# Row fetches by byte offsets, a tile in 12 and 14 sets, and a read-back with sets between its segments

## The chip, the core and the metric

One core of a Trainium2 chip runs the whole program. Its engines work side by side and meet only at semaphores: TensorE (PE in the profile), VectorE (DVE), ScalarE (ACT), GpSimd (POOL) and SyncE (SP). SyncE and ScalarE also issue direct DMA transfers, GpSimd issues indirect ones (a row of HBM for each of 128 partitions). The metric is device time in microseconds (us) of one execution; lower is better.

## What is computed

A layer of a graph network over 12,500 nodes of 256 features and 200,000 edges: a normalised row of each node goes through a weight matrix, is gathered along the edges, scaled and summed by destination; a linear attention over all nodes is added; then a mixture of 8 experts (the best 2 per node) is added.

```
xn = _layernorm(x, axis=-1)
HW = xn @ gnn_W
msgs = edge_vals[:, None] * HW[col]                       # row, col = src, dst
AHW = jax.ops.segment_sum(msgs, row, num_segments=12500)
x = x + (AHW + gnn_b) + linear_attention(xn)              # 8 heads of 32, elu(.)+1, bias mix_bproj
x = x + experts(_layernorm(x))                            # top 2 of 8, relu, 256 -> 512 -> 256
```

## The kernel before

**Sorting** (to about 677 us). The edges are sorted by destination block. A table of `xn @ gnn_W` is written to HBM (`h_table`, 12,544 rows of 1 KB), and the sorted edges are scattered to HBM as lists.

**Read-back** (about 680 to 776 us). The lists come back in 13 segments of 128 tiles (a tile is 128 edges of one destination block of 128 nodes). For each segment SyncE loads a list (L544), TensorE joins it (L1238), ScalarE copies it (`joined`, L965), TensorE turns it (L1280), ScalarE copies it again (`found`, L982). VectorE unpacks the segments in four parts, of 1, 4, 4 and 4 segments, into `records` (L1860 to L1877): the row to gather, the destination in the block, the weight. In this time ScalarE also fills the accumulator `acc` with the summed biases, in 14 pieces (L975), and TensorE turns the four weight matrices of the attention (L1267), which ScalarE copies (L972).

**Sets** (about 700 to 2770 us). 1,660 tiles are worked in 415 sets of four. For a tile, GpSimd gathers 128 rows of `h_table` into `message` (L757, one indirect DMA per tile, a ring of four sets); VectorE makes a selection matrix (`select`, L1815); TensorE multiplies the two (`aggregate`, L1258); VectorE adds the product to `acc` (L1823). GpSimd may be four sets ahead of TensorE: before set k it waits until set k - 4 is multiplied.

**Direct fetches.** In some sets the fourth tile is not gathered by GpSimd. SyncE or ScalarE fetches its 128 rows one by one, each by a direct DMA of 1 KB whose address comes from a register (L452), into `fetched`, two buffers for each queue. SyncE fetches one tile while 16 sets pass (25 tiles in all), ScalarE one while 20 pass (19 tiles). The row numbers stand in `fetch_row`, which is ready after the last segment; a queue loads eight of them into registers at a time (`TENSOR_LOAD`, L47), bounds them (L48) and issues eight transfers. `fetch_span` deals the rows out evenly: of span sets, the rows from 128·s/span to 128·(s + count)/span, rounded down, are fetched beside sets s to s + count.

**Attention beside the sets.** Sets 8 to 154 go with 49 context units, three sets each; sets 155 to 158 with the step between; sets 159 to 403 with 49 mix units, five sets each; 11 sets follow. In a context unit ScalarE takes `exp` and `relu` of the keys (L997, L998), copies the values (L1007), and then issues the unit's share of row transfers; in a mix unit `exp` and `relu` of the queries (L1026, L1027), then the rows. SyncE loads a unit's inputs (L563, in the mix also L575) once TensorE is through with the buffer, then issues its rows. Both queues work in order: what comes behind the rows of a unit waits until they are issued. VectorE needs ScalarE's `relu` within each unit (L1950), TensorE needs `v_sb` and SyncE's inputs.

**Experts** (about 2770 us to the end). Not touched by the change.

Of the kernel before, what the change touches and what calls it, by code (L numbers as in the profile page):

```python
# [50 lines left out]
def gps_layer(nc, x, src, dst, edge_weight, gnn_W, gnn_b, mix_Wq, mix_Wkv, mix_Wproj, mix_bproj,  # L51
# [4 lines left out]
    F32, BF16, I32 = mybir.dt.float32, mybir.dt.bfloat16, mybir.dt.int32  # L56
# [48 lines left out]
    AHEAD_SETS = 5  # L105
# [4 lines left out]
    SP_SPAN, SP_SET = 16, 27  # L110
    ACT_SPAN, ACT_SET = 20, 37
# [35 lines left out]
    with ExitStack() as whole:  # L147
# [16 lines left out]
        tiles_f = sb("tiles_f", [P, 4], F32)  # L164

# [34 lines left out]
        gnn_w = sb("gnn_w", [P, KC, C], F32, sorting)  # L200
        x_buf = sb("x_buf", [P, 14, 2 * C], F32, sorting)
# [30 lines left out]
        w_nat = lent[:, 0:8 * C].rearrange("p (a c) -> p a c", c=C)  # L232
        bias_in = lent[:, 8 * C:10 * C].rearrange("p (a c) -> p a c", c=C)
# [12 lines left out]
        bias_row = sb("bias_row", [P, C], F32, early)  # L246
# [71 lines left out]
        s_first_w = sem("s_first_w")  # L318
        s_x_group = [sem(f"s_x_group{i}") for i in range(3)]
# [170 lines left out]
        def _(sp):  # L490
# [23 lines left out]
            sp.wait_ge(s_block_dram, 16)  # L514
            for j in range(3, XGROUPS):
                sp.wait_ge(s_x_read, j - 2)
                load_group(j)
# [32 lines left out]
            sp.dma_start(bias_in[:, 0, :], gnn_b.partition_broadcast(P)).then_inc(s_first_w, 16)  # L550
            sp.dma_start(bias_in[:, 1, :], mix_bproj.partition_broadcast(P)).then_inc(s_first_w, 16)
# [25 lines left out]
            row_registers = [sp.alloc_register(f"row_{i}") for i in range(8)]  # L577
# [88 lines left out]
        def _(pool):  # L666
# [42 lines left out]
            def pass_gate():  # L709

                pool.sem_inc(s_passed, 1)
            pool.wait_ge(s_zeroed, 16 * G8)
# [12 lines left out]
            for slot in range(4):  # L725
                pool.wait_ge(s_xt_out[slot], STORED[slot])
                pool.wait_ge(s_h_out[slot], STORED[slot])
            pool.iota(iota_tile[:, :], [[1, TC]], base=0, channel_multiplier=0, allow_small_or_imprecise_dtypes=True)
# [19 lines left out]

            pool.wait_ge(s_first_w, 48)
            steps.done(pool.tensor_tensor(bias_row[:, :], bias_in[:, 0, :], bias_in[:, 1, :], ALU.add))  # L750
            steps.settle()
            pool.engine_nop().then_inc(s_late, 1)
# [82 lines left out]
        def _(act):  # L835
# [122 lines left out]


# [7 lines left out]
            def copy_weights():  # L967
                for i in range(4):
                    act.wait_ge(s_wt_psum, i + 1)
                    ps = bank[i][:, :].rearrange("p (k a n) -> p k a n", k=KC, a=2)  # L970
# [3 lines left out]
            def fill_acc(piece):  # L974
                act.activation(acc[:, 7 * piece:7 * piece + 7, 0:C], bias_row[:, :].unsqueeze(1).to_broadcast([P, 7, C]),  # L975
                               ACT.Copy).then_inc(s_acc_made, 1)
            join(0)
            for seg in range(RSEG):
                if seg + 1 < RSEG:
                    join(seg + 1)  # L980
                act.wait_ge(s_back_psum, seg + 1)
                act.activation(found_bf[:, seg * P:(seg + 1) * P, :],  # L982
                               bank[4 + seg % 2][:, :].rearrange("p (c t) -> p t c", c=PIECES), ACT.Copy).then_inc(s_back_out, 1)
                if seg == 1:
                    act.wait_ge(s_late, 3)
                if seg == 6:
                    copy_weights()
                for piece in range(2 * seg - 2, 2 * seg):
                    if 0 <= piece < NB // 7:
                        fill_acc(piece)  # L990


            def split_k(unit, first=False):
# [4 lines left out]
                act.activation(relu_kq[:, :], bank[4][:, :], ACT.Relu).then_inc(s_k_split, 1)  # L998
                act.wait_ge(s_v_psum, unit + 1)
# [9 lines left out]
            row_registers = [act.alloc_register(f"row_{i}") for i in range(8)]  # L1009
# [94 lines left out]
        def _(pe):  # L1104
# [156 lines left out]
            def turn_weights():  # L1261
                pe.wait_ge(s_tile_row, -(-TC // 512))
                pe.wait_ge(s_wload, 16 * 3)
                for i in range(4):
                    for k in range(KC):
                        for a in range(2):
                            last = nc.tensor.transpose(bank[i][:, (k * 2 + a) * P:(k * 2 + a + 1) * P],  # L1267
# [3 lines left out]
            for seg in range(RSEG):  # L1271
                if seg + 1 < RSEG:
                    join(seg + 1)
                if seg == 5:
                    turn_weights()
# [261 lines left out]
        def _(dve):  # L1537
# [274 lines left out]
            dve.wait_ge(s_late, 2)  # L1812
# [40 lines left out]

            for nth, (a, b) in enumerate(PARTS):
# [33 lines left out]
                elif nth == 1:  # L1888
# [10 lines left out]
            for k in range(AHEAD_SETS, RING):  # L1899
                set_turn(k)  # L1900
            dve.wait_ge(s_fetch_psum, 1)
            V.tensor_copy(fetch_row[:, :], bank[6][0:FETCHED, 0:P]).then_inc(s_fetch_row, 1)
# [33 lines left out]
            dve.wait_ge(s_late, 3)  # L1936
            dve.wait_ge(s_acc_made, NB // 7)
# [352 lines left out]
```

## Time and profile before

| | |
|---|---|
| median of three runs | 3810.78 us (3808.42 to 3811.88) |
| the profiled execution | 3811.51 us, of it 3809.8 us from the first to the last instruction |
| PE busy | 2769.5 us (73%) |
| DVE busy | 2526.5 us (66%) |
| POOL busy | 2461.2 us (65%) |
| ACT busy | 635.4 us (17%) |
| row transfers issued by SyncE and by ScalarE | 3200 and 2432, 1 KB each |

The shares are averages over stages with different limits. Issuing a DMA, loading a register and waiting for a semaphore are not counted as busy: a queue may be full although its engine reads as idle. In lists of groups the columns are line, engine, operation, output and input, count, then busy us and mean ns, then idle us just before them and what ended most of it; names that end in q (SPq, ACTq) are an engine's sequencer.

### The profile page before, as it was taken

Reading aid. Unit: us, or ns where it says so; the run is one execution under the profiler, and the core shown is the slowest. Engines: PE = TensorE matmul, PEld = TensorE weight load, DVE = VectorE, ACT = ScalarE, POOL = GpSimd, SP = SyncE. Lnnn points to the kernel's source line nnn. Section 1 sums busy time; section 2 is a strip of 40 time slices with the busy share of each in tenths; the row PEclk is TensorE's granted clock in tenths of the full one; section 3 lists DMA queues with packets and bytes.
Section 4 is the critical chain, followed back from the end, with each engine's and each line's share of the span. In section 5 each row is a group of like instructions: output and inputs, shape, how many; then the busy total and the mean of one; then the engine's idle time right before and its main releaser. Section 6 shows DMA issues by size and latency. Waiting matters only on the chain. (4 is left out here: it accounts for less than half of the span.)

```text
span 3809.8 us, 70900 instructions
## 1 busy us (share of the span) xinstructions
PE 2769.5 (73%) x16407; PEld 2275.1 (60%) x16408; DVE 2526.5 (66%) x6338; ACT 635.4 (17%) x1335; POOL 2461.2 (65%) x2387
## 2 busy tenths in 40 slices
PE   1457676577777776667666777666654999999998
PEld 1346666366556565555555555555432888888887
DVE  8999998355555555777777777777683544454444
ACT  8212222311111110000000000000032221122221
POOL 0047777477777777777777777777717378744444
PEclk9988778789999999998889888998877999999999
DMA  5957775644444444444444444444382455544443
GB/s 174 303 165 233 227 220 156 205 121 125 127 127 124 127 124 128 130 131 127 129 130 130 130 130 131 131 125 129 112 251 105 78 119 121 111 79 72 72 72 56
DMA packets 357535, 522.47 MB, mean 137 GB/s; under 512 B 59192, under 2 KB 278332, under 8 KB 357180
## 3 DMA queue, kind: packets, MB, share of 16 engines
q0 software_dynamic: 128832, 269.87, 28.1%
q1 hardware_dynamic: 172947, 191.01, 16.6%
q10 hardware_dynamic: 55401, 57.82, 4.9%
q8 instruction: 105, 1.72, 0.2%
q14 instruction: 250, 2.05, 0.2%
HBM read 378.21 MB, written 140.28 MB: 136 GB/s over the span
## 5 line engine op out<-in xcount | busy, mean ns | idle before, releaser
L757 POOL DMA_INDIRECT message<-h_table,records x1616 | 1552.3, 961 | 526.0 <-issue 508.1
L1258 PE MATMUL bank<-message,select 128*128 128x256 f32 x3232 | 925.6, 436 | 593.7 <-issue 306.9
L1258 PEld LDWEIGHTS bank<-message,select 128*128 128x128 f32 x3232 | 666.3, 215 | 811.1 <-issue 420.9
L1815 DVE TENSOR_SCALAR select<-iota_n,records 128x128 f32<-128x128 f32 x1660 | 595.7, 359 | 513.8 <-PE bank L1258 483.9
L1823 DVE TENSOR_TENSOR acc<-acc,bank 128x256 f32 x1660 | 683.0, 411 | 9.6 <-PE bank L1258 6.3
L801 POOL DMA_INDIRECT out<-acc,row_of x224 | 350.9, 1566 | 359.3 <-DVE acc L2235 234.8
L718 POOL DMA_INDIRECT lists<-placed,dest_i x300 | 351.0, 1170 | 316.3 <-ACT placed L934 222.6
L1498 PE MATMUL bank<-w,acc 128*128 x1792 | 407.6, 381 | 8.1 <-DVE acc L2219 7.8
L1485 PE MATMUL bank<-fx_t,acc 128*128 128x256 f32 x1792 | 408.1, 381 | 1.6 <-ACT fx_t L1078 1.6
L1485 PEld LDWEIGHTS bank<-fx_t,acc 128*128 128x128 f32 x1792 | 342.3, 191 | 49.2 <-issue 2.1
L1498 PEld LDWEIGHTS bank<-w,acc 128*128 128x128 f32 x1792 | 333.0, 191 | 51.1 <-issue 10.0
L2231 DVE TENSOR_TENSOR acc<-bank,table 128x256 f32<-128x256 f32 x224 | 84.5, 419 | 337.0 <-PE bank L1498 178.2
L790 POOL DMA_INDIRECT x_sorted<-acc,token_pos x196 | 191.3, 976 | 128.9 <-DVE acc L1934 69.5
L1026 ACT ACTIVATE exp_kq<-bank 128x512 f32<-128x512 f32 x49 | 29.3, 597 | 1153.6 <-PE bank L1369 1081.1
L2219 DVE TENSOR_SCALAR acc<-bank,table 128x256 f32<-128x256 f32 x448 | 190.6, 478 | 43.5 <-PE bank L1485 34.5
L1299 PE MATMUL bank<-w_cat,xt_in 128*128 128x256 f32 x784 | 193.3, 391 | 3.4 <-DMA xt_in<-xt_dram 3.4
L1078 ACT ACTIVATE fx_t<-bank 128x512 f32<-128x512 f32 x112 | 66.9, 597 | 644.1 <-PE bank L1472 644.1
L1299 PEld LDWEIGHTS bank<-w_cat,xt_in 128*128 128x128 f32 x784 | 157.0, 200 | 29.0 <-DMA xt_in<-xt_dram 4.5
L1950 DVE SCALAR_TENSOR_TENSOR act_kq<-exp_kq,relu_kq 128x512 f32<-128x512 f32 x98 | 67.9, 693 | 154.6 <-ACT relu_kq L998 147.4
L1996 DVE RECIPROCAL relu_kq<-exp_kq 128x512 f32<-128x512 f32 x49 | 164.3, 3353 | 1.7
L1167 PE MATMUL bank<-place_bf,hot_t 98*128 98x4 bf16 x1575 | 48.6, 165 | 133.5 <-DVE hot_t L1723 130.5
L1186 PE MATMUL bank<-hot_w,hot_q 128*128 128x128 bf16 x1575 | 139.3, 264 | 0.0
(315 smaller groups left out, 3405.0 us busy)
## 6 DMA issues: line engine op xcount, KB each, us to landing
fetched<-h_table SPq DMA_DIRECT2D x3200, 1.0 KB
fetched<-h_table ACTq DMA_DIRECT2D x2432, 1.0 KB
rows<-block_dram SPq DMA_DIRECT2D x75, 514.5 KB
acc<-x_sorted SPq DMA_DIRECT2D x112, 260.0 KB, 2.8
message<-h_table,records POOLq DMA_INDIRECT x1616
xt_in<-xt_dram SPq DMA_DIRECT2D x98, 256.0 KB
x_sorted<-blank_rows ACTq DMA_DIRECT2D x42, 390.0 KB
lists<-zeros_list SPq DMA_DIRECT2D x8, 1664.0 KB, 15.2
```

The lines of the kernel that those rows point to most:

```text
L718: pool.indirect_dma_start(out=lists, out_offset=Offset(ap=dest_i[:, c, i:i + 1], axis=0), in_=placed[:, c % 4, i * G8 * PIECES:(i + 1) * G ...
L757: pool.indirect_dma_start(out=message[:, k % SETS, j, :], out_offset=None, in_=h_table, in_offset=Offset(ap=records[:, k * SET + j, 0:1], ...
L790: pool.indirect_dma_start(out=x_sorted[half], out_offset=Offset(ap=token_pos[:, b, k:k + 1], axis=0), in_=acc[:, b, :], in_offset=None).th ...
L801: pool.indirect_dma_start(out=out, out_offset=Offset(ap=row_of[:, ring, j:j + 1], axis=0), in_=fy[:, slot, j, :], in_offset=None, compute_ ...
L1258: last = nc.tensor.matmul(ps, select[:, slot % 2, j, :], rows_of, start=True, stop=True)
L1299: last = nc.tensor.matmul(ps[:, u * C:(u + 1) * C], xt_in[:, half, k, u * P:(u + 1) * P], w_cat[:, k, cols:cols + C], start=(k == 0), stop ...
L1485: last = nc.tensor.matmul(bank[2 + 2 * slot + h // 2][:, h % 2 * 2 * P:(h % 2 + 1) * 2 * P], w1_now[:, slot, k * HID + h * P:k * HID + (h ...
L1498: last = nc.tensor.matmul(bank[6 + slot][:, j * C:(j + 1) * C], hid_t[:, slot, k, j * P:(j + 1) * P], w2_flat[:, ds(expert + k * C, C)], s ...
L1815: return V.tensor_scalar(select[:, k % 2, j, :], iota_n[:, :], records[:, k * SET + j, 1:2].bitcast(F32), records[:, k * SET + j, 2:3].bit ...
L1823: return V.tensor_tensor(to, to, ps, ALU.add)
L1996: steps.done(V.reciprocal(relu_kq[:, :], exp_kq[:, :]))
L2219: last = V.tensor_scalar(hid_t[:, slot, h, :], bank[2 + 2 * slot + h // 2][:, h % 2 * 2 * P:(h % 2 + 1) * 2 * P], table_flat[:, ds(expert ...
```

## The change

Five edits.

1. A row's register holds a byte offset: `fetch_row` is multiplied by 1024 on VectorE as it is made, `h_table` is addressed as bytes, and 16 registers are loaded at a time instead of 8.
2. SyncE fetches a tile in 12 sets instead of 16 (33 tiles), ScalarE in 14 instead of 20 (28 tiles): 61 tiles instead of 44, so GpSimd gathers 1,599 instead of 1,616.
3. In a context unit ScalarE issues the rows of the first set between `relu` and the copy of the values, the others behind the copy, as before.
4. The two bias rows are loaded and summed early in the sorting, and ScalarE fills `acc` ahead of the read-back: ten pieces after its last work of the sorting, four once the sorting's space is free.
5. All eight first sets stand between segments 3 and 10 of the read-back (before: five, from segment 7, and three behind it); the weights are turned behind the last segment instead of in segment 5, in other banks and from a buffer of their own.

```diff
-    AHEAD_SETS = 5
+    AHEAD_SETS, AHEAD_SEG = RING, 3
+    EARLY_FILL = 10
-    SP_SPAN, SP_SET = 16, 27
-    ACT_SPAN, ACT_SET = 20, 37
+    SP_SPAN, SP_SET = 12, 27
+    ACT_SPAN, ACT_SET = 14, 36
...
+        ROW_BYTES = 4 * C
+        h_bytes = h_table.rearrange("n c -> (n c)").bitcast(U8)
...
-            for a in range(first, end, 8):
-                n = min(8, end - a)
-                rows_at = load_offsets(eng, registers[0:n], fetch_row[at:at + 1, :], a, n, NB * P - 1)
+            for a in range(first, end, 16):
+                n = min(16, end - a)
+                byte_at = load_offsets(eng, registers[0:n], fetch_row[at:at + 1, :], a, n, (NB * P - 1) * ROW_BYTES)
                 for j in range(n):
-                    eng.dma_start(fetched[a + j:a + j + 1, queue, i % 2, :], h_table[ds(rows_at[j], 1), :]).then_inc(s_fetched[queue][i % 2], 16)
+                    eng.dma_start(fetched[a + j:a + j + 1, queue, i % 2, :].bitcast(U8),
+                                  h_bytes[ds(byte_at[j], ROW_BYTES)].unsqueeze(0)).then_inc(s_fetched[queue][i % 2], 16)
...
+            act.wait_ge(s_bias_row, 1)
+            act.wait_ge(s_hot_w, K)
+            act.wait_ge(s_looked, M)
+            act.wait_ge(s_found, M)
+            for piece in range(EARLY_FILL):
+                fill_acc(piece)
+            act.wait_ge(s_zeroed, 16 * G8)
+            act.wait_ge(s_blank, 16 * N_BLANKS)
+            act.wait_ge(s_proj, PAIRS)
+            act.wait_ge(s_tile_psum, -(-TC // 512))
+            for piece in range(EARLY_FILL, NB // 7):
+                fill_acc(piece)
...
-                split_k(unit, first=unit == 0)
-                if unit == 0:
-                    act.wait_ge(s_fetch_row, 1)
-                fetch_ahead(CONTEXT_FIRST + unit * CONTEXT_SETS, CONTEXT_FIRST + (unit + 1) * CONTEXT_SETS)
+                first_set = CONTEXT_FIRST + unit * CONTEXT_SETS
+
+                def first_rows():
+                    if unit == 0:
+                        act.wait_ge(s_fetch_row, 1)
+                    fetch_ahead(first_set, first_set + 1)
+                split_k(unit, first_rows, first=unit == 0)
+                fetch_ahead(first_set + 1, first_set + CONTEXT_SETS)
...
-                if RSEG - 1 - AHEAD_SETS <= seg < RSEG - 1:
-                    if seg == RSEG - 1 - AHEAD_SETS:
-                        pe.wait_ge(s_wt, 4)
-                    aggregate(seg - (RSEG - 1 - AHEAD_SETS), seg - (RSEG - 1 - AHEAD_SETS), True)
-            for k in range(AHEAD_SETS, RING):
-                aggregate(k, k, True)
+                if AHEAD_SEG <= seg < AHEAD_SEG + AHEAD_SETS:
+                    if seg == AHEAD_SEG:
+                        pe.wait_ge(s_tile_row, -(-TC // 512))
+                    aggregate(seg - AHEAD_SEG, seg - AHEAD_SEG, True)
             pe.wait_ge(s_back_out, RSEG)
             pe.wait_ge(s_fetch_f, 1)
             nc.tensor.transpose(bank[6][0:FETCHED, 0:P], fetch_f[:, :], ident[:, :]).then_inc(s_fetch_psum, 1)
+            pe.wait_ge(s_joined, RSEG)
+            turn_weights()
+            pe.wait_ge(s_wt, 4)
...
-                    dve.wait_ge(s_acc_made, NB // 7)
-                    set_turn(1)
-                elif nth == 2:
-                    for k in range(2, AHEAD_SETS):
-                        set_turn(k)
+                for k in (range(1, 3), range(3, 6), range(6, 7), range(0))[nth]:
+                    set_turn(k)
```

ScalarE's queue in a context unit before, from `exp` on; an ISA row is the bounding of loaded numbers or, ahead of a DMA, the arithmetic of an address:

```order
L997 ACTIVATE exp_kq<-bank 128x512 [waits s_k,s_k_psum]
L998 ACTIVATE relu_kq<-bank 128x512
L1007 ACTIVATE v_sb<-bank 128x4x128 [waits s_ctx,s_v_psum]
L47 TENSOR_LOAD fetch_row
L48 ISA
L452 REGISTER_ALU
L452 DMA fetched<-h_table 1x256
L452 ISA
L452 DMA fetched<-h_table 1x256
```

The same unit now:

```order
L1009 ACTIVATE exp_kq<-bank 128x512 [waits s_k,s_k_psum]
L1010 ACTIVATE relu_kq<-bank 128x512
L47 TENSOR_LOAD fetch_row
L48 ISA
L458 DMA fetched<-h_table 1x1024 x9
L1020 ACTIVATE v_sb<-bank 128x4x128 [waits s_ctx,s_v_psum]
L47 TENSOR_LOAD fetch_row
L48 ISA x2
L458 DMA fetched<-h_table 1x1024 x16
L47 TENSOR_LOAD fetch_row
L48 ISA
L458 DMA fetched<-h_table 1x1024 x2
```

Nothing stands between two row transfers any more; a load of 9 and its rows moved ahead of the copy of the values, and a unit of 27 rows takes three loads, of 9, 16 and 2 numbers.

SyncE's queue in a mix unit now (one of the first):

```order
L570 DMA xt_in<-xt_dram 128x512 [waits s_q_psum]
L582 DMA x_in<-in_x 128x2x256 [waits s_mix]
L47 TENSOR_LOAD fetch_row
L48 ISA x2
L458 DMA fetched<-h_table 1x1024 x16
...
L47 TENSOR_LOAD fetch_row
L48 ISA
L458 DMA fetched<-h_table 1x1024 x5
L570 DMA xt_in<-xt_dram 128x512 [waits s_q_psum]
```

Before, 40 rows in five loads of 8 stood behind the two input loads; now there are 53 or 54 in four loads, and the inputs of the unit after stand behind them.

TensorE at the end of the read-back before, from the last segment on:

```order
L1280 MATMUL bank<-ident_bf,joined 128x128 [waits s_back_out,s_joined]
L1280 MATMUL bank<-ident_bf,joined 128x128 x3
L1258 MATMUL bank<-message,select 128x256 [waits s_added,s_message1,s_select]
L1258 MATMUL bank<-message,select 128x256 x3
L1258 MATMUL bank<-message,select 128x256 [waits s_added,s_message2,s_select]
L1258 MATMUL bank<-message,select 128x256 x3
L1258 MATMUL bank<-message,select 128x256 [waits s_added,s_message3,s_select]
L1258 MATMUL bank<-message,select 128x256 x3
L1291 MATMUL bank<-ident,fetch_f 44x128 [waits s_fetch_f,s_back_out]
```

And now, from the last segment to the first set of the context:

```order
L1296 MATMUL bank<-ident_bf,joined 128x128 [waits s_back_out,s_joined]
L1296 MATMUL bank<-ident_bf,joined 128x128 x3
L1305 MATMUL bank<-ident,fetch_f 61x128 [waits s_fetch_f,s_back_out]
L1285 MATMUL bank<-ident,w_nat 128x128 [waits s_wload,s_joined]
L1285 MATMUL bank<-ident,w_nat 128x128 x11
L1285 MATMUL bank<-ident,w_nat 128x128 [waits s_wt]
L1285 MATMUL bank<-ident,w_nat 128x128 x3
L1275 MATMUL bank<-message,select 128x256 [waits s_message0,s_select,s_added,s_late,s_wt]
```

The three sets behind the last segment are gone from there, and the turning of the weights stands ahead of the first context set.

## Rows read from the trace of the kernel before

**Rows 1.** From the costliest groups of the page, columns as told above
```profile
L757 POOL DMA_INDIRECT message<-h_table,records x1616 | 1552.3, 961 | 526.0 <-issue 508.1
```
**Rows 2.** The gathers by source: min/median/max ns, first and last start us
```profile
L757 POOL DMA_INDIRECT message<-h_table,records x1616: 944/946/1465, 700.9 to 2763.5; - x180
```
**Rows 3.** Last work of a context and of a mix unit by source, columns as above
```profile
L1313 PE MATMUL bank<-v_sb,act_kq x388: 272/275/378, 782.5 to 1494.5; 128*128 128x129 f32 x194
L1391 PE MATMUL bank<-mix_w,act_kq x392: 379/379/634, 1537.1 to 2719.4; 128*128 128x256 f32 x196
```
**Rows 4.** Waits in the context stretch: us in total, times, longest us
```profile
ACT exp_kq L997 <- issue: 426.4, 34, 13.8
...
DVE act_kq L1950 <- ACT relu_kq L998: 147.4, 47, 7.4
```
**Rows 5.** Row transfers by source, line 452, all of them
```profile
L452 SPq MOVE fetched<-h_table x3200: 29/29/38, 774.8 to 2709.4; - x189
L452 SPq DMA_DIRECT2D fetched<-h_table x3200: 224/228/367, 774.9 to 2709.5; - x189
L452 SPq FUSED_REGOPS  x2800: 37/37/48, 775.3 to 2709.3; - x187
...
L452 ACTq DMA_DIRECT2D fetched<-h_table x2432: 234/235/551, 782.1 to 2641.3; - x188
```
**Rows 6.** Timeline within eight rows of SyncE, and of ScalarE: start us, us
```profile
1801.87 1.04 SPq L452 DMA_DIRECT2D fetched<-h_table  x3
...
1005.20 2.58 ACTq L452 DMA_DIRECT2D fetched<-h_table  x7
```
**Rows 7.** Register loads by source, line 47, all of them
```profile
L47 SPq TENSOR_LOAD <-fetch_row x400: 694/789/979, 773.7 to 2705.4; - x134
L47 ACTq TENSOR_LOAD <-fetch_row x346: 594/2002/2267, 781.0 to 2639.7; - x173
```
**Rows 8.** ScalarE's register loads by source, in four short stretches
```profile
L47 ACTq TENSOR_LOAD <-fetch_row x2: 772/812/852, 781.0 to 785.4; - x2
...
L47 ACTq TENSOR_LOAD <-fetch_row x2: 2005/2097/2189, 793.0 to 798.7; - x2
...
L47 ACTq TENSOR_LOAD <-fetch_row x1: 594/594/594, 848.5 to 848.5; - x1
...
L47 ACTq TENSOR_LOAD <-fetch_row x1: 778/778/778, 1560.6 to 1560.6; - x1
```
**Rows 9.** Timeline of SyncE, one context unit, then the input loads of a mix unit
```profile
801.80 12.22 SPq L452 DMA_DIRECT2D fetched<-h_table  x24
814.07 0.36 SPq L563 DMA_DIRECT2D xt_in<-xt_dram  x1
...
1808.72 0.41 SPq L575 DMA_DIRECT2D x_in<-in_x  x1
```
**Rows 10.** Timeline of GpSimd in the read-back: gathers with long idle times ahead of them
```profile
732.83 0.95 POOL L757 DMA_INDIRECT message<-h_table,records  x1 [11.61 <-issue]
...
753.14 0.95 POOL L757 DMA_INDIRECT message<-h_table,records  x1 [3.64 <-issue]
...
771.16 0.94 POOL L757 DMA_INDIRECT message<-h_table,records  x1 [3.14 <-issue]
```
**Rows 11.** Timelines of ScalarE, VectorE and TensorE in the read-back
```profile
691.95 0.60 ACT L965 ACTIVATE joined<-bank 128x512 bf16<-128x512 f32 x1 [33.15 <-PE bank L1238]
...
738.14 0.35 DVE L1815 TENSOR_SCALAR select<-iota_n,records 128x128 f32<-128x128 f32 x1 [15.45 <-ACT acc L975]
...
720.85 2.17 PE L1267 MATMUL bank<-ident,acc 128*128 128x128 f32 x16
...
756.96 0.54 DVE L1860 TENSOR_SCALAR records<-found 128x512 int32<-128x512 int32 x1 [2.06 <-ACT found L982]
...
762.22 0.84 DVE L1877 TENSOR_TENSOR records<-records,found_a 128x512 int32<-128x512 int32 x1
```
**Rows 12.** The filling of the accumulator by source
```profile
L975 ACT ACTIVATE acc<-bias_row x14: 1690/1715/1767, 703.0 to 735.5; 128x1792 f32<-128x1792 f32 x14
```

More of the change, by code:

```diff
@@ L164, in gps_layer @@
         tiles_f = sb("tiles_f", [P, 4], F32)
+        bias_row = sb("bias_row", [P, C], F32)
         sorting = ExitStack()
@@ L245, in gps_layer @@
         row_ok = sb("row_ok", [P, 2, P], F32, early)
-        bias_row = sb("bias_row", [P, C], F32, early)
+        w_nat = sb("w_nat", [P, 8, C], F32, early)
         message = sb("message", [P, SETS, SET, C], F32, early)
@@ L318, in gps_layer @@
         s_first_w = sem("s_first_w")
+        s_bias = sem("s_bias")
+        s_bias_row = sem("s_bias_row")
         s_x_group = [sem(f"s_x_group{i}") for i in range(3)]
@@ L575, in bring_x @@
                     sp.dma_start(x_in[:, pair % 2, :, :], x_pairs[pair:pair + 1, :, :, :].rearrange("a p u c -> p (a u) c")).then_inc(s_x_in[pair % 2], 16)
-            row_registers = [sp.alloc_register(f"row_{i}") for i in range(8)]
+            row_registers = [sp.alloc_register(f"row_{i}") for i in range(16)]
             def fetch_ahead(first, end):
@@ L711, in pass_gate @@
                 pool.sem_inc(s_passed, 1)
+            pool.wait_ge(s_bias, 32)
+            pool.tensor_tensor(bias_row[:, :], bias_in[:, 0, :], bias_in[:, 1, :], ALU.add).then_inc(s_bias_row, 1)
             pool.wait_ge(s_zeroed, 16 * G8)
@@ L957, in _, with fill_acc @@
                     copy_h(g + 1)
+            def fill_acc(piece):
+                act.activation(acc[:, 7 * piece:7 * piece + 7, 0:C], bias_row[:, :].unsqueeze(1).to_broadcast([P, 7, C]),
+                               ACT.Copy).then_inc(s_acc_made, 1)
+            act.wait_ge(s_bias_row, 1)
[10 more added lines that the diff above has]
+                fill_acc(piece)
             found_bf = found[:, :, :].rearrange("p t w -> p (t w)").bitcast(BF16).rearrange("p (t c) -> p t c", c=PIECES)
@@ L969, in copy_weights @@
                     act.wait_ge(s_wt_psum, i + 1)
[L970 removed]
+                    ps = bank[[4, 5, 7, 4][i]][:, :].rearrange("p (k a n) -> p k a n", k=KC, a=2)
                     into = [w_cat[:, :, 2 * C:3 * C], w_cat[:, :, 0:C], w_cat[:, :, C:2 * C], wp_t[:, :, :]][i]
                     act.activation(into.rearrange("p k (a n) -> p k a n", a=2), ps, ACT.Copy).then_inc(s_wt, 1)
[L974 to L976 removed]
             join(0)
@@ L983, in _, with split_k @@
                                bank[4 + seg % 2][:, :].rearrange("p (c t) -> p t c", c=PIECES), ACT.Copy).then_inc(s_back_out, 1)
[L984 to L993, printed above, removed]
+            copy_weights()
+            def split_k(unit, between, first=False):
                 act.wait_ge(s_k_psum, unit + 1)
@@ L998, in split_k @@
                 act.activation(relu_kq[:, :], bank[4][:, :], ACT.Relu).then_inc(s_k_split, 1)
+                between()
                 act.wait_ge(s_v_psum, unit + 1)
@@ L1008, in _ @@
             act.wait_ge(s_late, 2)
-            row_registers = [act.alloc_register(f"row_{i}") for i in range(8)]
+            row_registers = [act.alloc_register(f"row_{i}") for i in range(16)]
             def fetch_ahead(first, end):
@@ L1261, in turn_weights @@
             def turn_weights():
-                pe.wait_ge(s_tile_row, -(-TC // 512))
                 pe.wait_ge(s_wload, 16 * 3)
                 for i in range(4):
+                    if i == 3:
+                        pe.wait_ge(s_wt, 1)
                     for k in range(KC):
                         for a in range(2):
-                            last = nc.tensor.transpose(bank[i][:, (k * 2 + a) * P:(k * 2 + a + 1) * P],
+                            last = nc.tensor.transpose(bank[[4, 5, 7, 4][i]][:, (k * 2 + a) * P:(k * 2 + a + 1) * P],
                                                        w_nat[:, 2 * i + a, k * P:(k + 1) * P], ident[:, :])
@@ L1898, in _ @@
             V.engine_nop().then_inc(s_fetch_f, 1)
-            for k in range(AHEAD_SETS, RING):
+            for k in range(RING - 1, RING):
                 set_turn(k)
             dve.wait_ge(s_fetch_psum, 1)
-            V.tensor_copy(fetch_row[:, :], bank[6][0:FETCHED, 0:P]).then_inc(s_fetch_row, 1)
+            V.tensor_scalar(fetch_row[:, :], bank[6][0:FETCHED, 0:P], float(ROW_BYTES), None, ALU.mult).then_inc(s_fetch_row, 1)
             def block_stats(first_block, j):
```

21 lines of the change are left out of this document (7 added, 14 removed).

## The prediction, made before the changed kernel ran

> **What bounds the kernel now.** I began with the stage that the change touches, sets 0 to 414, and asked of each engine whether it ever waits there. GpSimd's groups come first: 1,616 gathers of 961 ns [rows 1], the last of which starts at 2763.5 us [rows 2]. The gather at 771.16 is the last with a long idle time ahead of it [rows 10]. It is the first of set 10, ahead of which 40 tiles lie, so 1,575 follow, and the pitch is (2763.5 − 771.2) / 1575 = 1.265 us, the gather itself and 0.3 us. So GpSimd sets the pace of everything behind the read-back. A context unit lasts (1494.5 − 782.5) / 48 = 14.83 us, a mix unit (2719.4 − 1537.1) / 48 = 24.63 [rows 3].
>
> Then who comes next. A busy share says nothing here, because issuing a DMA and loading a register don't count as busy. The list of waits does: in the context stretch `exp` starts late by ScalarE's own queue ("issue") 34 times, 426 us in all, and VectorE waits 147 us in 47 of 49 units for the `relu` behind it [rows 4]. An engine that starts late through its own issue is full. So ScalarE is nearly as long as GpSimd there, and the change gives it 43% more rows.
>
> **What a row costs.** A row is a MOVE of 29 ns, a transfer of 224 to 235, and between two rows an address instruction of 37 [rows 5]. Three transfers of SyncE take 1.04 us: (1.04 − 0.224) / 2 = 0.408 us from row to row. Seven of ScalarE take 2.58: (2.58 − 0.234) / 6 = 0.391 [rows 6]. In the new order the address instruction is gone. I take away its 37 ns and as much again for the gap that it makes, an estimate: 0.408 − 0.29 leaves 0.118 us a row beside MOVE and transfer, for that instruction and two or three gaps. That gives 0.333 us on SyncE and 0.316 on ScalarE. The transfer is the same 1 KB, now written as 1,024 bytes; no row shows such a one. My bounds are the old pitch (nothing saved) and 0.29, which is MOVE plus transfer with no gap; below that the transfer itself would have to become quicker.
>
> **What a load costs.** SyncE's 400 loads of eight take 0.69 to 0.98 us, ScalarE's 346 loads a median of 2.00 [rows 7]. They differ in where they start. By `fetch_span` SyncE's shares are 24 or 40 rows, so it always starts at a multiple of eight. ScalarE's first unit has 19 rows: its loads at rows 0 and 8 take 0.77 and 0.85 us; the second unit's, of eight too, at rows 19 and 27, take 2.19 and 2.01. The fifth unit ends with four numbers from row 92: 0.594. A load of two, from no multiple of four, takes 0.778 [rows 8]. So a load that starts at a row divisible by four costs about 0.4 + 0.05n (0.594 for four, 0.81 for eight), any other (2.1 − 0.778) / 6 = 0.22 a number, about 0.4 + 0.2n; I use 0.2. Sixteen numbers: 1.2 us or 3.6. No load of sixteen is in the trace; both lines are carried from eight. What is left over of an aligned load past a multiple of four I price at 0.2 each.
>
> Around a load lie its bounding and a slower first transfer. 24 rows of SyncE, with two loads between them, take 12.22 us [rows 9]: (12.22 − 0.224 − 23 × 0.408) / 2 − 0.789 = 0.52. I take 0.5 per load on both queues.
>
> **Context, part 2 and 3 of the change.** ScalarE's unit after: 3/14 of 128 = 27.4 rows × 0.316 = 8.7. Three loads (9, 16 and 2 in the order shown): of their 27.4 numbers 19.0 fall to loads that start at no multiple of four, by laying out the 49 units (101 of 147 loads), and 8.4 to others: 3 × 0.4 + 19.0 × 0.2 + 8.4 × 0.05 = 5.4, with left-overs 5.6. Rests 3 × 0.5 = 1.5, `exp` and `relu` 0.55 of the queue's time. Sum 16.35. The same sum for before: 19.2 × 0.391 = 7.5, loads of 8, 8 and 3 about 5, 1.5, 0.55: 14.55, beside 14.83 measured, as it should be for a queue that is nearly full. GpSimd would now need only (12 − 0.46) × 1.265 = 14.6. So ScalarE becomes the bound: 49 × (16.35 − 14.83) = **+74 us**. Moving a set's rows ahead of the copy of the values covers its wait for TensorE, but makes the copy and what needs `v_sb` later by some 3.5 to 5 us; I cost it at nothing, because VectorE's `relu` still comes first and TensorE has the rest of the unit; if that cover is gone, the unit grows by part of it, 1 us being 49. SyncE has 32 rows in two aligned loads: 10.7 + 2.4 + 1.0 + 0.36 for the input [rows 9] = 14.5, not the bound.
>
> **Mix, part 2.** SyncE's unit after: 5/12 of 128 = 53.35 rows × 0.333 = 17.8. Its shares no longer start at multiples of eight: 0, 53, 106, 32, 85, 10 and so on. 108 of 196 loads start at no multiple of four, with 29.2 numbers a unit, 24.2 on the others: 4 × 0.4 + 29.2 × 0.2 + 24.2 × 0.05 = 8.65, with left-overs 8.75. Rests 2.0, two input loads 0.36 + 0.41 = 0.8 [rows 9]. Sum 29.35, against 24.63 now, where it had 16.3 + 5 × 1.3 + 0.8 = 23.6. The unit's inputs stand behind the rows of the unit ahead, so TensorE then waits for `xt_in`, its sets come late and GpSimd stops for lack of a free `message`. ScalarE: 45 × 0.316 + 7.7 + 1.6 + 0.55 = 24.1; GpSimd 19.2 × 1.265 = 24.3. So SyncE sets the pace: 48 × (29.35 − 24.63) = **+227 us**. It enters the mix ahead of TensorE, since the context leaves it slack and four sets of rows lie between; that lead is spent first: **−20 us**, an estimate (four sets, about 5 us each).
>
> **Read-back, parts 4 and 5.** GpSimd idles 11.61, 3.64 and 3.14 us there, less 0.3 each: 17.5 [rows 10]. The first stall is VectorE's wait of 15.45 us for ScalarE's filling of `acc` [rows 11], in pieces of 1.715 us [rows 12]; ScalarE idles 33.15 us ahead of 691.95, which covers the ten early ones, 17 us; the weights' turning, 2.17 us on TensorE, no longer lies among the segments, and the last part of the lists still takes VectorE from 756.96 to 763 [rows 11]. That part, the segments and the copies of the weights ahead of the first context set can still outlast GpSimd's lead of four sets, 16 × 1.265 = 20 us; I leave 4.5 of the 17.5 for it: **−13 us**. Bounds: 0 and −17.5. The fetched tiles spare GpSimd 17 gathers, 21.5 us, but only where it is the bound, so here they count nothing.
>
> **Sum.** The profiled execution took 3811.5 us, 0.7 above the median. 3811.5 − 13 + 74 + 227 − 20 = 4079.5. I forecast **4080**. With 0.15 or 0.25 us a number on unaligned loads a ScalarE unit moves by 0.95 and a SyncE unit by 1.46 us, 117 us in all; with 0.03 us more or less a row by 0.8 and 1.6, another 117. These alone give about 3960 to 4200.
>
> **The rivals.**
>
> *The queues keep up* (the other side). GpSimd stays the bound and does 17 gathers less: 3811.5 − 13 − 21.5 = 3777. It needs ScalarE's unit at 14.6 and SyncE's at 24.3 or below: a row pitch of (14.6 − 7.65) / 27.4 = 0.25 and (24.3 − 11.55) / 53.35 = 0.24. For it: no row shows a transfer by bytes, and its address may be cheaper within the transfer too. Against it: 224 ns of transfer and 29 of MOVE are 0.253 without any gap. Long loads in bulk would do as well, but 8 unaligned numbers show no bulk. Chance 0.10.
>
> *SyncE's loads stay cheap.* No row of SyncE shows an unaligned start; the slow ones are all ScalarE's. If it is ScalarE that is slow, and not the start, SyncE's unit is 17.8 + 4.3 + 2.0 + 0.8 = 24.9, nearly GpSimd's, and 3811.5 − 13 + 74, with a few us of the mix that the lead takes up, is about 3875. Against: ScalarE's own aligned loads cost what SyncE's do. Chance 0.09.
>
> *A row costs what it did* (the edit doesn't do what it says): context 27.4 × 0.391 + 7.65 = 18.4, mix 53.35 × 0.408 + 11.55 = 33.3: −13 + 175 + 416 − 20, about 4370. Against: an instruction really is gone from between the rows. Chance 0.04.
>
> *Every load is slow.* If aligned loads lost their bulk at sixteen, all at 0.2 a number, SyncE's units are 10.7 + 0.8 + 6.4 + 1.4 = 19.3 and 17.8 + 1.6 + 10.7 + 2.8 = 32.9: −13 + 219 + 397 − 20, about 4395. SyncE's 400 loads of eight at 0.789 speak against it. Chance 0.02. The Trainium skill ("Runtime: NRT & Kernel Launch", Instruction fetch mechanics) puts a register load at about 200 ns a register even in bulk, which would give this time; the trace agrees for unaligned starts alone.
>
> *Gains and losses cancel*, with a pitch near 0.255: chance 0.03.
>
> **How the numbers follow.** My forecast keeps 0.72. The rivals above 4220 and those at or under 3811 hold 0.19, so the range is 3870 to 4220, which takes in SyncE's cheap loads. About 0.2% is what a measurement of this kernel can tell from no change. Faster 0.10, same 0.03, slower 0.87.
>
> **What would show it.** In the trace of after: rows of line 458 at a pitch of 0.33 and 0.32; loads of line 47 up to 3.6 us on both queues, 1.2 where they start at a multiple of four; the context at about 16.4 us a unit and the mix at 29.3; long idle times of GpSimd put down to TensorE's `aggregate`; TensorE waiting for `xt_in` in the mix, VectorE for `relu` in the context; GpSimd's set 10 near 758 us in place of 771. I am wrong if gathers follow one another at 1.265 throughout, or if SyncE's loads in the mix stay near 1.2 us.

## The result

The changed kernel takes 4048.83 us (median of 5 runs, 4045.47 to 4050.21), beside 3808.50 us for the kernel before (5 runs, 3805.74 to 3811.88): a ratio of 1.0629, 95% interval 1.0614 to 1.0643. It is slower by about 240 us, where 4080 us was forecast. The profiled execution has a span of 4043.7 us.

The price of a load and of a row, line 47 and line 458 by source (operation, output and input, count, then min/median/max in ns, first and last start in us), all of them and then SyncE's loads in two short stretches of the mix. The rows answer to [rows 5, 7]:

```profile
L47 ACTq TENSOR_LOAD <-fetch_row x309: 605/2136/3915, 761.7 to 2944.0; - x155
L47 SPq TENSOR_LOAD <-fetch_row x297: 779/1265/3769, 754.6 to 2967.0; - x149
...
L47 SPq TENSOR_LOAD <-fetch_row x3: 3577/3634/3648, 1547.7 to 1566.2; - x3
...
L47 SPq TENSOR_LOAD <-fetch_row x3: 1252/1264/1282, 1580.6 to 1594.4; - x3
...
L458 SPq DMA_DIRECT2D fetched<-h_table x4224: 224/228/397, 756.3 to 2970.4; - x192
L458 ACTq DMA_DIRECT2D fetched<-h_table x3584: 234/235/553, 763.0 to 2950.3; - x200
```

All six loads in the two stretches are of sixteen numbers. The first three belong to the unit that starts at row 74 and begin at rows 74, 90 and 106; the others begin at rows 0, 16 and 32. The same queue, the same length, a factor of 2.9. SyncE, which had no slow load before, now has them as ScalarE has. A transfer costs what it did. What lies between two of them is read from stretches without a load, 14 rows of SyncE and 12 of ScalarE on the timeline (start us, us, ..., count):

```profile
1552.16 4.43 SPq L458 DMA_DIRECT2D fetched<-h_table  x14
...
1014.92 3.81 ACTq L458 DMA_DIRECT2D fetched<-h_table  x12
```

(4.43 − 0.224) / 13 = 0.323 us from row to row on SyncE, (3.81 − 0.235) / 11 = 0.325 on ScalarE, before 0.408 and 0.391 [rows 6].

SyncE's timeline over the first of these units, from one input load to the next:

```profile
1546.81 0.36 SPq L570 DMA_DIRECT2D xt_in<-xt_dram  x1
1547.22 0.44 SPq L582 DMA_DIRECT2D x_in<-in_x  x1
1551.77 27.81 SPq L458 DMA_DIRECT2D fetched<-h_table  x54
1579.63 0.36 SPq L570 DMA_DIRECT2D xt_in<-xt_dram  x1
```

32.8 us for a unit that had lasted 24.63 [rows 3]; it is one of the longest, since three of its four loads start badly. What it does to the stages, as the last work of a context and of a mix unit by source, then GpSimd's gathers:

```profile
L1330 PE MATMUL bank<-v_sb,act_kq x388: 272/422/555, 767.1 to 1553.8; 128*128 128x129 f32 x194
...
L1408 PE MATMUL bank<-mix_w,act_kq x392: 379/379/634, 1592.5 to 2958.8; 128*128 128x256 f32 x196
...
L762 POOL DMA_INDIRECT message<-h_table,records x1599 | 1535.9, 961 | 781.0 <-issue 753.8
```

A context unit now takes (1553.8 − 767.1) / 48 = 16.39 us, a mix unit (2958.8 − 1592.5) / 48 = 28.46. A gather is as long as in [rows 1], 961 ns, but GpSimd idles 781 us between them instead of 526. It has become the one that waits. The profile puts 753.8 of these down to "issue", not to TensorE's `aggregate` as the prediction expected. But the times tell: 68 gathers stand more than 1 us idle, each the first of a set, and 67 of them start 0.80 us behind the end of the last `aggregate` of the set four before. GpSimd waits there for a free `message`, as forecast.

Who waits for whom, from the list of waits (us in total, times, longest us), first of the context and then of the mix:

```profile
ACT exp_kq L1009 <- issue: 439.8, 42, 11.9
...
DVE act_kq L1963 <- ACT relu_kq L1010: 180.1, 49, 6.0
...
DVE acc L1995 <- ACT relu_kq L1044: 430.8, 48, 14.6
...
PE bank L1386 <- DMA xt_in<-xt_dram: 285.6, 43, 12.5
```

In the context ScalarE's `exp` is late by its own queue 42 times in 49, before 34 [rows 4]. In the mix TensorE waits for `xt_in` in 43 units, the input that stands behind SyncE's rows. VectorE waits in the mix for ScalarE's `relu` as well; part of that is only the echo of TensorE's own lateness, part is ScalarE, as e4 shows below.

The read-back on GpSimd's timeline (in brackets the idle time ahead), which answers to [rows 10]:

```profile
694.92 1.02 POOL L762 DMA_INDIRECT message<-h_table,records  x1 [12.54 <-DVE records L1895]
...
755.00 0.95 POOL L762 DMA_INDIRECT message<-h_table,records  x1 [0.30 <-issue]
760.62 0.95 POOL L762 DMA_INDIRECT message<-h_table,records  x1 [4.67 <-issue]
```

48 gathers run without a stop from 694.92 on; one stall of 4.67 us is left, ahead of set 12. Set 10 starts at 745.75 us, earlier than the 758 that the prediction named: the first gather is earlier, and the stall that is left falls behind set 10.

### The profile page after: what moved, and what is told of

Same layout as the page of the kernel before. It is cut to its first block and busy times, and to the rows that moved or that the text cites. A ratio compares the mean times of both kernels' runs of the same rounds, so it can differ in the third digit from the quotient of the medians.

```text
span 4043.7 us, 69846 instructions
## 1 busy us (share of the span) xinstructions
PE 2838.3 (70%) x16403; PEld 2351.9 (58%) x16408; DVE 2522.9 (62%) x6338; ACT 639.1 (16%) x1335; POOL 2542.4 (63%) x2370
## 3 DMA queue, kind: packets, MB, share of 16 engines
q1 hardware_dynamic: 174995, 192.06, 15.4%
## 5 line engine op out<-in xcount | busy, mean ns | idle before, releaser
L762 POOL DMA_INDIRECT message<-h_table,records x1599 | 1535.9, 961 | 781.0 <-issue 753.8
L1275 PE MATMUL bank<-message,select 128*128 128x256 f32 x3198 | 875.3, 425 | 80.8 <-DVE acc L1840 54.1
L1275 PEld LDWEIGHTS bank<-message,select 128*128 128x128 f32 x3198 | 685.2, 219 | 231.6 <-DVE select L1832 99.5
L1386 PE MATMUL bank<-xt_in,w_cat 128*128 128x256 f32 x392 | 152.7, 557 | 285.7 <-DMA xt_in<-xt_dram 285.6
L1995 DVE TENSOR_TENSOR acc<-acc,bank 128x512 f32<-128x512 f32 x49 | 33.7, 688 | 430.9 <-ACT relu_kq L1044 430.8
L1386 PEld LDWEIGHTS bank<-xt_in,w_cat 128*128 128x128 f32 x392 | 103.9, 277 | 323.2 <-DMA xt_in<-xt_dram 303.3
L1330 PE MATMUL bank<-v_sb,act_kq 128*128 128x129 f32 x388 | 95.1, 422 | 214.2 <-ACT v_sb L1020 213.8
L1330 PEld LDWEIGHTS bank<-v_sb,act_kq 128*128 128x128 f32 x388 | 82.4, 313 | 232.5 <-issue 232.5
```

The source lines that it names most:

```text
L762: pool.indirect_dma_start(out=message[:, k % SETS, j, :], out_offset=None, in_=h_table, in_offset=Offset(ap=records[:, k * SET + j, 0:1], ...
L1275: last = nc.tensor.matmul(ps, select[:, slot % 2, j, :], rows_of, start=True, stop=True)
L1386: last = nc.tensor.matmul(bank[4][:, o * C:(o + 1) * C], w_cat[:, k, 2 * C + o * P:2 * C + (o + 1) * P], xt_in[:, half, k, :], start=(k == ...
```

## The experiments

The theory is the prediction's: the address at which a load of row numbers starts sets its price, these loads fill ScalarE's queue in the context and SyncE's in the mix, and a full queue sets the pace. The rivals: the number of rows alone is too much for the queues; the two queues disturb one another; the read-back is where time went.

**Loads at multiples of four (e1).**

```
-  fetch_rows(..., P * (first - begins) // span, P * (end - begins) // span)
+  fetch_rows(..., 4 * (P // 4 * (first - begins) // span), 4 * (P // 4 * (end - begins) // span))
```

> The changed kernel, with one edit: the rows of a tile are dealt out to the sets in multiples of four, so every register load starts at a number divisible by four. The same 61 tiles, rows and byte offsets, nearly the same number of loads. Theory (the start of a load sets its price): no load over 1.5 us; ScalarE's context unit falls from 16.4 to about 13.2 us and SyncE's mix unit from 28.5 to about 24.3, GpSimd sets the pace again with 14.6 and 24.4 us a unit, and the time is about 3808 - 15 (read-back) - 21 (17 gathers less) = 3765 to 3785. Rival (the number of rows is too much for the queues, or a load is slow by its length): loads of sixteen stay at 3.6 us somewhere or the units stay at 16 and 28, time 3950 to 4050.

Measured: 3766.78 us, ratio 0.9899 (0.9883 to 0.9916). Loads, and the units' last work, by source:

```profile
L47 SPq TENSOR_LOAD <-fetch_row x297: 555/1227/1435, 757.8 to 2678.2; - x149
L47 ACTq TENSOR_LOAD <-fetch_row x284: 581/1202/1441, 765.3 to 2660.2; - x142
...
L1330 PE MATMUL bank<-v_sb,act_kq x388: 272/275/349, 770.2 to 1465.6; 128*128 128x129 f32 x194
...
L1408 PE MATMUL bank<-mix_w,act_kq x392: 379/379/634, 1511.1 to 2676.7; 128*128 128x256 f32 x196
```

No load is over 1.44 us, though SyncE issues as many as before the edit; units of 14.49 and 24.28 us, GpSimd's pace. One line about where shares end moves 282 us. The number of rows is not too much.

**The address alone (e5).** e1 with the list stored one word further along, so that each load begins one word past a multiple of four:

```
-  fetch_row = sb("fetch_row", [FETCHED, P], I32, early)
+  fetch_row = sb("fetch_row", [FETCHED, P + 4], I32, early)      # written from word 1 on
-  load_offsets(eng, registers[0:n], fetch_row[at:at + 1, :], a, n, ...)
+  load_offsets(eng, registers[0:n], fetch_row[at:at + 1, :], a + 1, n, ...)
```

> The kernel of e1 (rows dealt out in multiples of four), with the list of byte offsets one word further along in its memory: the same loads, sizes, rows and order, but every load now starts one word past a multiple of four. Theory (the address at which a load starts sets its price): all loads of sixteen go from 1.2 to 3.6 us on both queues; SyncE's context unit sums to 18.9, its mix unit to 32.3, so the time is about 3767 + 49 x (18.9 - 14.5) + 48 x (32.3 - 24.3) - 20 = 4345 (4250 to 4400). Rival (what made the loads of e1 cheap is their number or where a share begins, not the address): 3765 to 3790.

Measured: 4375.96 us, ratio 1.1494 (1.1471 to 1.1517); 4345 was expected.

```profile
L47 SPq TENSOR_LOAD <-fetch_row x297: 1128/3555/3836, 755.8 to 3296.2; - x149
L47 ACTq TENSOR_LOAD <-fetch_row x284: 1184/3656/3939, 763.3 to 3273.3; - x142
...
L1330 PE MATMUL bank<-v_sb,act_kq x388: 272/275/554, 769.3 to 1677.9; 128*128 128x129 f32 x194
...
L1408 PE MATMUL bank<-mix_w,act_kq x392: 379/379/634, 1726.1 to 3288.1; 128*128 128x256 f32 x196
```

Same loads, same lengths, same order as e1, and the median goes from 1.2 to 3.6 us on both queues. Units of 18.93 and 32.54 us, against sums of 18.9 and 32.3. (The expectation took off 20 us for a lead of SyncE. Here SyncE's queue is full in the context too, and the first mix unit's input is issued at 1706.5 us, only 3.2 us before TensorE uses it: no lead.) This shows the cause: neither the engine, the count nor the length, but the start.

**The two queues apart (e2, e3, e4).** The spans put back, both, ScalarE's only, SyncE's only; all else as in the changed kernel:

```
e2: SP_SPAN, SP_SET = 16, 27   ACT_SPAN, ACT_SET = 20, 37
e3: SP_SPAN, SP_SET = 12, 27   ACT_SPAN, ACT_SET = 20, 37
e4: SP_SPAN, SP_SET = 16, 27   ACT_SPAN, ACT_SET = 14, 36
```

> The changed kernel with a tile in 16 and 20 sets, as before: byte offsets, loads of up to sixteen, the early filling and the sets between the segments remain. Theory: neither queue is the bound (about 11.5 us a context unit, 18.4 a mix unit), GpSimd gathers at 1.265 us throughout, and what is left of the change is the read-back: 15 to 20 us, so 3788 to 3795. Rival (parts 3 to 5 give back later what they gain in the read-back): 3805 to 3812.

> The changed kernel with ScalarE's tiles in 20 sets as before and SyncE's in 12. Theory: only the mix is long. Context about 14.7 us a unit, mix about 28.5, time about 3790 + 185 = 3960 to 3980. Rival (ScalarE's rows take part in the mix too, or the DMA engines are shared by both): the mix falls below 27 and the time below 3920.

> The changed kernel with SyncE's tiles in 16 sets as before and ScalarE's in 14. Theory: only the context is long, by ScalarE alone: 16.4 us a unit, the mix at 24.5 to 24.8 since ScalarE's unit there sums to 24.5; time about 3790 + 80 = 3865 to 3890. Rival (SyncE's rows lengthen the context as well): the context falls to 15.5 or less, time near 3830.

Measured: e2 3786.47 us, 0.9949 (0.9932 to 0.9966); e3 3974.99, 1.0444 (1.0426 to 1.0461); e4 3903.58, 1.0256 (1.0239 to 1.0274). e3 is as the theory has it: SyncE's rows alone cost the mix. e2 is 1.5 us below its range: the read-back, byte offsets and longer loads alone gain 20 us. Not all of it is the read-back, though. Of e2, the context units' last work:

```profile
L1330 PE MATMUL bank<-v_sb,act_kq x388: 272/275/349, 765.4 to 1467.3; 128*128 128x129 f32 x194
```

Beside the kernel before [rows 3] the first unit is 17 us earlier, and the 48 others are 10 us shorter, 14.62 us each in place of 14.83. ScalarE's `exp` is late by its own queue there 3 times, 23 us in all, before 34 times and 426 us [rows 4]: the shorter queue gains as well. (The profiled execution of before took 3811.5 us, 5 more than the median beside e2, so the two terms add up to more than 20.) Of e3, the units' last work:

```profile
L1330 PE MATMUL bank<-v_sb,act_kq x388: 272/275/422, 769.6 to 1466.4; 128*128 128x129 f32 x194
...
L1408 PE MATMUL bank<-mix_w,act_kq x392: 379/379/634, 1511.0 to 2889.6; 128*128 128x256 f32 x196
```

14.52 us in the context and 28.72 in the mix. e4 lies 14 us above its range. Its units' last work, what ScalarE's `exp` waits for in the mix, and a stretch of ScalarE on the timeline, its rows and each `exp`:

```profile
L1330 PE MATMUL bank<-v_sb,act_kq x388: 272/422/554, 768.1 to 1558.9; 128*128 128x129 f32 x194
...
L1408 PE MATMUL bank<-mix_w,act_kq x392: 379/379/634, 1597.5 to 2822.5; 128*128 128x256 f32 x196
...
ACT exp_kq L1043 <- issue: 1042.9, 42, 27.7
...
1991.49 0.60 ACT L1043 ACTIVATE exp_kq<-bank 128x512 f32<-128x512 f32 x1 [26.81 <-issue]
...
2000.58 11.45 ACTq L458 DMA_DIRECT2D fetched<-h_table  x29
2012.13 0.60 ACT L1043 ACTIVATE exp_kq<-bank 128x512 f32<-128x512 f32 x1 [19.56 <-PE bank L1386]
...
2016.32 20.90 ACTq L458 DMA_DIRECT2D fetched<-h_table  x46
2037.33 0.60 ACT L1043 ACTIVATE exp_kq<-bank 128x512 f32<-128x512 f32 x1 [24.11 <-issue]
...
2041.49 24.03 ACTq L458 DMA_DIRECT2D fetched<-h_table  x46
2065.61 0.60 ACT L1043 ACTIVATE exp_kq<-bank 128x512 f32<-128x512 f32 x1 [27.20 <-issue]
```

The context is 16.47 us, as expected. The mix is 25.52 where I had put ScalarE's mean unit, 24.5, level with GpSimd's 24.45 (19.33 gathers at 1.265). It is ScalarE's queue that sets this pace, in long units and in short ones. `exp` is late by its own queue in 42 of the units, and in all 49 it starts 0.1 us behind the last row of the unit before, with TensorE's product ready. (At 2012.13 the row names TensorE, whose product had ended 0.3 us before.) ScalarE's units are uneven, and the short ones stay short: from `exp` to `exp` these three last 20.6, 25.2 and 28.3 us, of which the first is well below GpSimd's 24.45; by the prices of loads and rows they are 20.3, 24.7 and 27.4. So a short unit does make up for a long one, and the mean is what counts. It was the wrong mean: 24.5 takes in the last unit, for which only 10 rows are left; the other 48 sum to 24.9 by the same prices, above GpSimd. The remaining 0.6 us a unit no price covers, and no run takes it apart.

**The address instruction (e6).** e1 with row numbers, as before the change:

```
-  byte_at = load_offsets(..., (NB * P - 1) * ROW_BYTES)
-  eng.dma_start(fetched[...].bitcast(U8), h_bytes[ds(byte_at[j], ROW_BYTES)].unsqueeze(0))
+  rows_at = load_offsets(..., NB * P - 1)
+  eng.dma_start(fetched[...], h_table[ds(rows_at[j], 1), :])
```

> The kernel of e1 with row numbers in the registers, as before the change, so an address instruction stands between two rows again. Theory (a row then costs 0.408 and 0.391 us): SyncE's mix unit sums to 53.35 x 0.408 + 4.3 + 2.0 + 0.8 = 28.9 and ScalarE's context unit to 27.4 x 0.391 + 2.4 + 1.3 + 0.55 = 15.0, so the time is about 3767 + 48 x 4.6 - 20 + 49 x 0.5 = 3990 (3940 to 4010). Rival (with cheap loads the queues keep up without byte offsets): 3765 to 3800.

Measured: 4129.34 us, ratio 1.0849 (1.0831 to 1.0867). Slower as expected, and beyond the range that I gave. By source, and a wait of TensorE in the context:

```profile
L458 SPq FUSED_REGOPS  x3927: 37/37/48, 758.5 to 3048.5; - x197
...
L1329 PE MATMUL bank<-v_sb,act_kq x388: 272/275/553, 769.4 to 1590.7; 128*128 128x129 f32 x194
...
L1407 PE MATMUL bank<-mix_w,act_kq x392: 378/380/635, 1635.1 to 3039.1; 128*128 128x256 f32 x196
...
PE bank L1315 <- DMA xt_in<-xt_dram: 215.7, 47, 6.4
```

The mix, 29.25 us, is near its sum of 28.9. The context, 17.11 us, is SyncE's: TensorE waits there for `xt_in`. I had summed ScalarE's unit alone (15.0); SyncE's is 32 × 0.408 + 2.4 + 1.0 + 0.4 = 16.9. With it, 48 × (17.11 − 14.49) + 48 × (29.25 − 24.28) = 364 us over e1, beside 363 measured. So the 37 ns instruction between two rows, with its gaps, is worth about 363 us once 61 tiles are fetched. Each of the two, byte offsets and good starts, is needed.

**Rows behind the copy (e7).** The third edit undone:

```
-  split_k(unit, first_rows, first=unit == 0)
+  split_k(unit, lambda: None, first=unit == 0)
+  first_rows()
   fetch_ahead(first_set + 1, first_set + CONTEXT_SETS)
```

> The changed kernel without its third edit: in a context unit all of ScalarE's rows stand behind the copy of the values, the first set's rows as a load of their own. Theory (the rows ahead of the copy cover ScalarE's wait for TensorE, 2.4 us a unit): the context grows from 16.4 us a unit by 1 to 2.4, time 4095 to 4165. Rival (the place of the copy doesn't matter): 4040 to 4055. A second rival (the copy comes too late with the edit, TensorE waits 214 us for it in the changed kernel): faster than 4040.

Measured: 4049.58 us, ratio 1.0638 (1.0620 to 1.0656), which can't be told from the changed kernel. The list of waits, context:

```profile
ACT exp_kq L1009 <- issue: 685.9, 46, 16.6
DVE act_kq L1964 <- ACT relu_kq L1010: 337.9, 47, 10.2
```

The first rival holds. The second falls with it: TensorE's wait of 214 us for the copy is gone from the list of waits here, and nothing is gained, since the copy was late by the queue that sets the pace anyway. A full queue comes to the copy late, when TensorE has long made the values, so there is no wait left to cover; with the rows ahead of it or behind it the unit is the same queue's sum (16.51 and 16.39 us).

**No early filling (e9).** e2 with all 14 pieces where the last four stood:

```
-  EARLY_FILL = 10
+  EARLY_FILL = 0
```

> The kernel of e2 (spans of 16 and 20 sets) with none of the 14 pieces of the accumulator filled early: all of them stand where the last four stood, after the sorting's space is free and ahead of the first joined segment. Theory (the early filling is worth its ten pieces on the path to the first gather, 1.6 us each): the first gather starts 14 to 17 us later, at about 710 us, and the time is 3786 + 14 to 17 = 3800 to 3804. Rival (GpSimd loses the gain again behind the last segment, so most of the read-back's 20 us came from the sets between the segments): 3786 to 3793.

Measured: 3805.25 us, ratio 0.9991 (0.9982 to 1.0000), against e2's 0.9949; 3800 to 3804 was expected. ScalarE's and GpSimd's timelines:

```profile
682.54 22.32 ACT L965 ACTIVATE acc<-bias_row 128x1792 f32<-128x1792 f32 x14 [24.84 <-PE bank L1261]
...
710.34 1.02 POOL L762 DMA_INDIRECT message<-h_table,records  x1 [28.17 <-DVE records L1895]
...
776.38 0.94 POOL L762 DMA_INDIRECT message<-h_table,records  x1 [4.42 <-issue]
```

The first gather starts 15.4 us later than in the changed kernel, and 9.4 later than before the change. Behind it the gathers run as in the changed kernel, with one stall of 4.42 us, where before there were 11.61, 3.64 and 3.14 [rows 10]. So the stalls are gone without the early filling too: by the new order of the sets, or because the filling no longer stands among the segments; no run takes the two apart. What that saves is lost again ahead of the first gather, where the filling stands in this run, and the first context unit's last work starts at 782.3 us, as before the change (782.5). Of the runs here the read-back gains only where the filling lies in ScalarE's idle time.

**A version that beats both (e8).** e1 with ScalarE's tiles in 12 sets as well, used from set 29 on, and up to 32 numbers a load:

```
-  ACT_SPAN, ACT_SET = 14, 36
+  ACT_SPAN, ACT_SET = 12, 29
-  for a in range(first, end, 16):
+  for a in range(first, end, 32):
```

> The kernel of e1 with ScalarE's tiles in 12 sets as well (66 tiles in all) and up to 32 registers a load. Theory: SyncE's units sum to 13.2 and 22.8 us, ScalarE's context unit to 14.4, just below GpSimd's 14.55, so 5 gathers less are worth 6 us: 3757 to 3763. Rival (ScalarE's context unit is uneven or held up and takes over): 3775 to 3800.

Measured: 3761.52 us, ratio 0.9883 (0.9867 to 0.9900). It is 46 us faster than the kernel before and 287 faster than the changed one; e1's interval overlaps with its own, so its 5 us over e1 are likely, not shown.

## Why the prediction was right

By stages, each worked out from the two profiles; the terms add up to the difference of the spans, 233.9 us:

| stage | forecast | measured | from |
|---|---|---|---|
| to the first context unit | −13 | −15.4 | 767.1 − 782.5 |
| context | +74 | +75 | 48 × (16.39 − 14.83) |
| step between the stages | | −4 | 1592.5 − 1553.8, before 1537.1 − 1494.5 |
| mix, with SyncE's lead | +207 | +184 | 48 × (28.46 − 24.63) |
| behind the mix | 0 | −5.5 | 4043.7 − 2958.8, before 3809.8 − 2719.4 |

- **Loads.** Sixteen numbers were priced at 1.2 or 3.6 us by carrying two lines on from eight; their medians, by the row at which they start, are 1.24 and 3.64 on SyncE, 1.30 and 3.76 on ScalarE. That SyncE shows no slow load in the trace of before was a matter of its shares of 24 and 40, as e1 and e5 show; the rival in which its loads stay cheap falls.
- **Context.** The sum for ScalarE, 16.35, met 16.39, in part by luck: its rows came at 0.325 us in place of 0.316, which is 0.25 us a unit and 12 us in all, so another term was put too high by as much; which, no run shows. The third edit was costed at nothing, and e7 measures nothing, for another reason than I gave: it is the queue's own lateness that covers the copy.
- **Mix.** Here the forecast was 23 us too high. SyncE's queue is read from the inputs that it issues in the mix, and its lead from when TensorE uses them:

```profile
L570 SPq DMA_DIRECT2D xt_in<-xt_dram x49: 359/363/363, 1546.8 to 2937.4; - x49
...
L1386 PE MATMUL bank<-xt_in,w_cat x392: 379/634/797, 1566.4 to 2943.4; 128*128 128x256 f32 x196
```

  (2937.4 − 1546.8) / 48 = 28.97 us a unit, where 29.35 was forecast; that is 18 of the 23 us. It is the price of a row that was off: SyncE's rows follow one another at 0.323 us in place of 0.333, which is 0.5 us a unit, 26 us in all; its loads of sixteen, 0.04 us dearer than forecast, take a part of that back. With the row's price the unit sums to 28.8, and e3 has 28.72. The lead was rightly named: the first unit's input is issued 19.6 us before TensorE uses it, the sixth's 4.0 (1689.8 and 1693.8). The first unit's last work comes 45.7 us behind its input, the last unit's 21.4, so the lead was worth 24 us in place of 20. The 4 us between the stages are not part of it: the step takes 38.7 us, and 38.6 in e4, where SyncE's tiles are as before.
- **ScalarE in the mix** was said to be no bound, 24.1 against 24.3. In the changed kernel SyncE hides it. e4 shows that the statement was wrong: the 24.1 is a mean that takes in the last unit with its 10 rows. By the prediction's own prices the 48 others sum to 24.5, over GpSimd's 24.3.
- **Read-back.** The stalls fell from 17.5 to about 4.4 us, as forecast, but the reason given for the first was wrong. It was put down to VectorE's wait for the filling, which ends at 738.14 us [rows 11]; the gather behind the stall starts at 732.83 already [rows 10]. What it waits for is the product of set 0, on TensorE before:

```profile
730.03 1.99 PE L1258 MATMUL bank<-message,select 128*128 128x256 f32 x8 [0.96 <-ACT wp_t L972]
```

  Set 0 stood behind segment 7 and the turned weights. So the early filling was not what removed this stall, and e9, without it, has no such stall either; that the forecast of the stalls came out is luck in part. What the sum left out is that the first gather starts 6.0 us earlier, at 694.92 in place of 700.95. SyncE's first list is issued at 677.95, where before it stood behind the two bias loads until 679.85; that is 1.9 of the 6.0, and about 1.0 of these is a sorting that ended earlier. The rest lies in loading and joining the first lists, and no run takes it apart. I had priced the edit where the loads and the filling went, not where they came from. The first context unit starts only 15.4 us earlier, since the weights are turned ahead of its first set (on TensorE from 751.73, the set at 756.04 us).
- **Behind the mix.** GpSimd's last gather starts 39.5 us behind the last mix unit, before 44.1. Where it is not the bound it runs further ahead of TensorE: at that unit's last work 32 gathers are left, and 36 in e1 with the same 61 tiles; four at 1.265 us are 5. I had not priced that.
- **The other side.** It asked for a row at 0.24 to 0.25 us; rows are at 0.323 and 0.325. The 17 gathers less are worth 20 us, near the 21.5 that was put there, once the queues keep up: e2 to e1.

## What to carry to other kernels

An engine's queue has a length of its own, which no busy share shows: add up issues, loads and their rests for a unit of work, and compare that with the pace of the engine that bounds. Before giving a queue more to do, look where its register loads start, and cut the shares so that all start well; take the mean over full units, since a short last one can hide that the queue is the bound. Ask of a stall which event ended it: a wait that ends later than the stall isn't its cause. A filling or loading moved into idle time of the same engine gains what it took on the path.

## What the runs showed of the hardware

- A load of sixteen registers from the on-chip list takes about 1.2 us where it starts at a multiple of four words and 3.6 to 3.8 one word further on, on SyncE and ScalarE alike (e1 and e5). In the changed kernel, starts one, two and three words past a multiple of four cost ScalarE the same for sixteen registers, medians of 3.75 to 3.77. A load of 32 numbers with a good start takes about 2.1 us (e8, SyncE, whose loads are mostly of 32):

```profile
L47 SPq TENSOR_LOAD <-fetch_row x157: 701/2068/2231, 757.7 to 2637.0; - x157
```

- A transfer whose register holds a byte offset is issued as quickly as one by row number, 224 to 235 ns; what it saves is the instruction ahead of it.
- TensorE's granted clock, a mean over stretches at 2.4 and at 1.2 GHz as a share of the first, was 0.94 in the context before, 0.82 in the changed kernel, where TensorE is not busy for 214 of 786 us, and 0.95 in e1, where it is 171 of 695. The two rows are of the table by stretches (busy us and count of PE, PEld, DVE, ACT, POOL, then the clock, DMA share and GB/s), the changed kernel and e1:

```profile
767.00:1553.00 786.00, 572.05 (x2312) 488.50 (x2313) 384.21 (x1207) 80.86 (x144) 537.93 (x560) 0.82 0.39 115
```

```profile
770.00:1465.00 695.00, 524.35 (x2312) 428.28 (x2311) 385.37 (x1203) 80.87 (x144) 527.37 (x550) 0.95 0.43 127
```

The edit of e1 touches no work of TensorE, so the lower clock comes with the full queue. What it costs by itself no run shows; since `exp` is late by ScalarE's own queue in 42 of the 49 context units, it is probably little.
